# Query items kept in memory by column of head: loads of 8 KB rows, and one store for each of three parts

## What is computed

```python
x = x + attn(layernorm(x))
x = x + ffn(layernorm(x))

# attn
qkv = h @ Wqkv                      # 512 query columns, 16 key, 16 value
scores = einsum('bqhd,bkd->bhqk', q, k) * 16 ** -0.5
scores = where(causal, scores + slopes * (pos_k - pos_q), NEG_INF)
probs = softmax(scores)
attn = einsum('bhqk,bkd->bqhd', probs, v) @ Wo

# ffn: base layer, and the two best of 8 experts of rank 16
result = h @ W_base.T + b_base
delta  = sum over the two best experts of route_w * (h @ A_e.T) @ B_e.T
```

## Time and profile before

| what | value |
|---|---|
| time, median of 3 runs | 699.22 us (697.58 to 699.97) |
| the profiled execution | 698.62 us, span of its instructions 696.9 us |
| busy: PE / DVE / ACT / POOL | 673.5 / 552.3 / 360.7 / 216.5 us |
| granted clock of TensorE | 0.999 of full speed |
| loads of items (L504) | 96 DMAs of 128 KB, median 5.4 us from issue to landing |
| stores of items (L489) | 16 DMAs of 384 KB, median 4.4 us |

### The profile page before, as it was taken

How to read it: one execution, slowest core, us unless ns; L and a number is a source line. 1 busy time by engine, 2 the same in 40 slices (tenths; PEclk the granted TensorE clock), 3 DMA queues, 4 the chain that set the end, 5 groups by cost and what they waited for, 6 DMA issues and landing times.

```text
span 696.9 us, 13297 instructions
## 1 busy us (share of the span) xinstructions
PE 673.5 (97%) x4326; PEld 308.8 (44%) x4326; DVE 552.3 (79%) x1794; ACT 360.7 (52%) x519; POOL 216.5 (31%) x366
## 2 busy tenths in 40 slices
PE   7899999999999999999999999999999999999997
PEld 5444344544454444435443343343333455555553
DVE  6798989787989889898988989989881375656565
ACT  3325656666657667666666666666668411111111
POOL 0054323233341614234252231422431412222220
PEclk9999999999999999999999999999999999999999
DMA  9778108081411443080144843325200189600001
GB/s 243 161 146 141 42 6 143 28 153 27 152 61 44 65 85 118 2 132 34 40 70 89 117 75 67 52 46 95 48 18 34 64 123 177 151 31 31 30 31 60
DMA packets 43000, 56.32 MB, mean 81 GB/s; under 512 B 6697, under 2 KB 26281, under 8 KB 42801
## 3 DMA queue, kind: packets, MB, share of 16 engines
q1 hardware_dynamic: 40344, 51.27, 37.1%
q10 hardware_dynamic: 2592, 4.26, 1.8%
HBM read 35.72 MB, written 19.79 MB: 80 GB/s over the span
## 4 chain that ended last, share of the span: by engine, by line
PE 83%; DVE 9%; DMA 2%; ACT 2%; issue 1%; SPq 1%; POOL 0%; DVEq 0%; ACTq 0%; POOLq 0%
PE psum L784 20%; PE psum L736 18%; PE psum L766 13%; PE psum L812 8%; PE psum L834 7%; PE psum L682 7%; PE psum L763 5%; DVE psum L1170 3%; PE psum L829 2%; PE psum L844 2%; ACT work L976 2%; DVE negm L1175 1%; DMA x_sb<-in_x 1%; PE psum L821 1%; DMA arena<-q_dram 1%
## 5 line engine op out<-in xcount | busy, mean ns | idle before, releaser
L976 ACT ACTIVATE work<-psum 128x1024 f32<-128x1024 f32 (+1 forms) x320 | 288.9, 942 | 125.1 <-PE psum L766 106.6
L1170 DVE CUSTOM_DVE_ANT_0 psum<-psum,future 128x384 f32<-128x384 f32 (+3 forms) x512 | 238.0, 514 | 14.9 <-PE psum L736 12.8
L736 PE MATMUL psum<-k_op,arena 106*128 106x512 bf16 (+3 forms) x768 | 212.2, 328 | 9.3 <-DVE negm L1170 3.1
L1175 DVE TENSOR_REDUCE negm<-psum 128x1 f32<-128x512 f32 x256 | 168.7, 688 | 15.4 <-PE psum L736 11.2
L1345 POOL TENSOR_SCALAR_AFFINE_SELECT work<-work 128x512 f32<-128x512 f32 x128 | 81.5, 637 | 296.8 <-ACT work L976 296.8
L784 PE MATMUL psum<-work,v_op 128*32 128x512 f32 (+3 forms) x1536 | 163.4, 498 | 0.6 <-POOL work L1345 0.4
L766 PE MATMUL psum<-arena,k_op 109*128 109x512 bf16 (+3 forms) x640 | 157.4, 316 | 1.0 <-ACT work L976 0.8
L736 PEld LDWEIGHTS psum<-k_op,arena 106*128 106x128 bf16 x768 | 69.1, 97 | 127.9 <-DVE negm L1170 39.7
L682 PE MATMUL psum<-arena,wqkv_sb 128*128 128x256 f32 (+3 forms) x240 | 84.5, 452 | 1.2 <-ACT arena L894 1.2
L763 PE MATMUL psum<-arena,k_op 116*128 116x128 bf16 x512 | 84.1, 221 | 0.9 <-ACT work L976 0.9
L766 PEld LDWEIGHTS psum<-arena,k_op 109*128 109x128 bf16 x640 | 59.6, 98 | 43.1 <-ACT work L976 14.7
(11 more groups left out here) (90 smaller groups left out, 456.1 us busy)
## 6 DMA issues: line engine op xcount, KB each, us to landing
arena<-q_dram SPq DMA_DIRECT2D x96, 128.0 KB, 5.4
o_dram<-o_sb SPq DMA_DIRECT2D x32, 256.0 KB
q_dram<-arena SPq DMA_DIRECT2D x16, 384.0 KB, 4.4
arena<-o_dram SPq DMA_DIRECT2D x32, 128.0 KB, 4.5
arena<-rcp_dram SPq DMA_DIRECT2D x32, 128.0 KB, 4.8
out<-wqkv_sb ACTq DMA_DIRECT2D x16, 256.0 KB, 2.0
work<-in_x SPq DMA_DIRECT2D x3, 1024.0 KB, 16.9
x_sb<-in_x SPq DMA_DIRECT2D x8, 256.0 KB, 5.1
```

What stands on the lines that cost most here:

```text
L736: last = nc.tensor.matmul(bank[:, a * width:(a + 1) * width], q_op[0:ROW_MAX, bass.ds(col, P)], k_op[0:ROW_MAX, b, k0:k0 + width], start=T ...
L976: nc.scalar.activation(probs[:, n % 4, heads * hp:heads * (hp + 1), 0:w], src, ACT.Exp).then_inc(exp_done, 1)
L1170: last = nc.vector.tensor_tensor_reduce(keys, keys, future[:, CH - width:CH], -1.0, 3e38, ALU.add, ALU.min, negm[:, late, 0, j * QT + t:j ...
L1175: nc.vector.tensor_reduce(dst, psum[:, bank, 0:len(js) * width].rearrange("p (a k) -> p a k", a=len(js)), AX_X, ALU.max, negate=True).then ...
```

## The change

`q_dram` gets the shape (chunk, part, group, column, head, token). A load then takes one run of 8 KB (eight heads of 1 KB) for each of its 16 partitions, where it took eight runs of 1 KB. A store must put row h * 16 + d of the tile at place (d, h), which one DMA per part does: its memory side counts 8 heads, 16 columns, 512 tokens. The head part is issued as soon as ACT has written it, the other two after the split. The semaphore `q_stored` counts 48 for an item instead of 16.

```diff
-        q_dram = nc.dram_tensor("q_dram", (NCH, 3, D, CH), BF16, kind="Internal").ap()
+        q_dram = nc.dram_tensor("q_dram", (NCH, 3, PAIRS, DH, 2 * UH, CH), BF16, kind="Internal").ap()
...
             def store_queries(n):
                 c, m = Q_ITEMS[n]
-                if n < 2:
-                    sp.wait_ge(q_split_v, n + 1)
-                else:
-                    sp.wait_ge(q_split_p, n - 1)
                 if n:
-                    sp.wait_ge(q_stored, 16 * n)
-                sp.dma_start(q_dram[c, :, P * m:P * (m + 1)].rearrange("a r q -> r a q"),
-                             qpart[:, n % 4]).then_inc(q_stored, 16)
+                    sp.wait_ge(q_stored, 48 * n)
+                sp.wait_ge(q_hi_ready, n + 1)
+                for a in range(3):
+                    if a == 1:
+                        if n < 2:
+                            sp.wait_ge(q_split_v, n + 1)
+                        else:
+                            sp.wait_ge(q_split_p, n - 1)
+                    sp.dma_start(q_dram[c, a, m].rearrange("d h q -> h d q"), qpart[:, n % 4, a]).then_inc(q_stored, 16)
             def load_queries(n):
...
-                sp.wait_ge(q_stored, 16 * (n + 1))
+                sp.wait_ge(q_stored, 48 * (n + 1))
...
                 for r, (a, _) in enumerate(PARTS):
-                    sp.dma_start(q_op_pairs[DH * r:DH * (r + 1), c % 2, g].rearrange("d (h q) -> d h q", q=CH),
-                                 q_dram[c, a, g * P:(g + 1) * P].rearrange("(h d) q -> d h q", d=DH)).then_inc(q_in[n % 2], 16)
+                    sp.dma_start(q_op_pairs[DH * r:DH * (r + 1), c % 2, g],
+                                 q_dram[c, a, g].rearrange("d h q -> d (h q)")).then_inc(q_in[n % 2], 16)
...
                 if n >= 4:
-                    act.wait_ge(q_stored, 16 * (n - 3))
+                    act.wait_ge(q_stored, 48 * (n - 3))
```

## The result

| | before | changed |
|---|---|---|
| median of 6 runs each, same chip | 699.38 us (697.51 to 699.97) | 704.09 us (703.43 to 706.38) |
| ratio, 95% interval | | 1.0084 [1.007, 1.0098] |
| the profiled execution | 698.62 us, span 696.9 | 703.71 us, span 702.0 |
| granted clock, mean | 0.999 | 0.995 |

A forecast was written before the change was run, and what follows sets the result against it. PE bounds the kernel, busy 673.5 of 696.9 us. Item 0's +0.8 and the chain's +3.1 (4.5 - 0.4 - 1.0) make +3.9 on 698.6: 702.5, or 703.0 for a median; range 698.7 to 706.5.

The forecast's parts named there:

- slower: Whole kernel: chance 0.61 that the change makes it slower, against 0.33 for same and 0.06 for faster.
- the sum of 3.9: Whole kernel: +0.8 us at item 0 and +3.1 at the chain to unit 1, added to the profiled execution's 698.6.
- Loads, no change: Query item loads: 16 partitions limit them, not row size, so 8 KB rows cost 0; rival of faster loads 0.09.
- Stores use eight engines: Item stores: outermost count 8 gives eight engines, 165 GB/s, share near 0.5; rival that stores keep all engines 0.16.
- The price of a store, +1.5: Each item store takes 1.5 us longer, between +1.1 and +1.7; 4.5 us for three in the chain.
- the lower price of +1.1: Each item store at 165 GB/s takes 2.4 us against 1.3; rival of cheap stores, mostly covered, 0.17.
- crowd: Item stores: if eight engines crowd the same SBUF places, the rate is nearer 133 GB/s, +1.7 us per store.
- The place: Stores of items 3, 4 and 5 stand in series before unit 1's maximum rows; PE stands still 3.1 us there.
- the room before 71.47: Unit 1's maximum rows: 0.4 us of room between their load's landing and PE's first scores, taken off the loss.
- The cover of 1.0: Unit 1: DVE has other work at 72.42, so 1.0 us of PE's delay is taken as covered.
- Item 0, +0.8: Start: item 0's store ends 0.8 us later; PE already waits for these loads, so it is paid in full.
- Later items, 0: Ten more stores, one in a step and not in a chain, ahead of an early unit's maximum rows: cost 0.

The follow-up runs named there:

- long loads alone: Kernel before with W_q's columns permuted, so one store of 128 rows per item serves loads with 8 KB rows: 698.6 us, ratio 0.9995.
- the padded kernel: Kernel before, its order by head and 1 KB loads, a pad row per head and three 8 by 16 by 512 stores per item: 704.11 us, ratio 1.0074.
- The kernel kept busy: Changed kernel plus 14 matmuls, later overwritten, in front of unit 1's late scores to fill PE's wait: 703.4 us, ratio 1.007.
- that with 17 matmuls: Changed kernel plus 17 matmuls, later overwritten, in front of unit 1's late scores: 703.16 us, ratio 1.0054.
- one extra store: Kernel before plus one 384 KB store that nothing reads, between store 5 and unit 1's maximum rows: 699.48 us, ratio 1.0012.
- three stores on all engines: Kernel before, its layout and loads, each item stored by three DMAs of 128 rows, head part first: 698.9 us, ratio 1.0006.
- the broken chain: Changed kernel with unit 1's maximum rows moved ahead of store 5: 700.1 us, ratio 1.0014.

## Why the prediction held, step by step

The median of 704.09 lies 1.1 us above the 703.0, in the range, and slower was the likeliest side. In the profiled executions 5.1 us stand against the sum of 3.9.

- **Loads, no change: right.** The six landings of item 0 go from 2.9 to 5.6 us after issues that take 2.65 us in all, so they are 0.98 us apart against 1.04, at 145 GB/s. The kernel with long loads alone is as fast as before, and loads to 32 partitions move 1.6 to 1.8 times as much at the same share, which bears the reason out.
- **Stores use eight engines: right.** The share is 0.47 to 0.48, the padded kernel shows the same, and it alone gives the loss.
- **The price of a store, +1.5: too high, in a part that was guessed.** The rate that the lower price of +1.1 was worked out from (165 GB/s) is what is seen (154 to 165), so the eight blocks don't crowd. Taken were 4.5 us for the three, measured are 3.3 (up to 3.9 in the other executions): 0.67 and 0.71 where data moves under the issues, 1.94 at store 5. So the first two cost less than even the lower price, which isn't explained, and the third more: there the issues, costed at 0.38 and as lying under data, count in full, at 0.58 each.
- **The place: right.** The chain starts 0.5 us later (load 2 at 50.07 against 49.57), takes 3.3 more, and its end is 3.8 later (73.32 against 69.50). Its load then lands 1.60 us on, which makes the room before 71.47 - 69.50 - 1.60 = 0.37 us, predicted 0.4. Of 3.8, less 0.37, 3.45 arrive at PE. Breaking the chain at store 5 takes away most of the loss.
- **The cover of 1.0: right in kind, 0.8 in size.** The kernel kept busy shows 3.47 us turned into 2.66, that with 17 matmuls 3.7 into 2.9, and one extra store a wait of 0.75 turned into 0.02.
- **Item 0, +0.8: the store's price came, its way to PE did not.** From the end of the split to the first load it is 2.74 us before (20.38 to 23.12) and 3.41 in the changed kernel (19.60 to 23.01), so the store costs +0.7. But the split ended 0.8 us earlier in this execution, and the last load landed 5.6 us after its issue against 5.9; so the first slot is 0.47 us earlier, and PE's wait there 0.83 instead of 1.42. The late slots wait 0.5 for a query item instead and are 0.2 late. The step that failed is "paid in full": it took the end of the split and the landing of the loads as fixed. Why the split came earlier isn't shown, and the change need not be the reason: the kernel with long loads alone, which stores as before, has it at 19.58 too, and its first slot 0.3 us ahead of the changed kernel's. The first slot varies from 30.50 to 32.49 in the executions with before's stores and loads, and from 30.97 to 33.14 in those of the changed kernel and its edited versions at full clock.
- **The clock: left out.** The sum took PE's standing still at its length less the cover. Measured is 0.2 at the start, plus 3.25 less 0.8 of wait, plus 2.5 at the 1.2 GHz level: 5.15. Without the clock it is 2.65, 1.25 less than forecast: the stores were 1.2 too dear and item 0 0.6, while the chain began 0.3 later than unit 0's scores show and the cover was 0.2 smaller. That the sum came near is luck: two kinds of error had opposite signs. The trace of before couldn't show it here, since PE had no wait of this size in the run after its start.
- **Later items, 0: right.** The lag is constant from 82 us to the end.

## What to carry to other kernels

When a DMA is reshaped, count the outermost rows of both sides: here a store whose memory side counts 8 ran on half the engines, although it read 128 partitions. Change the order of the data where it is made (here the weights' columns) rather than in the DMA, and merge loads so that each fills more partitions (the loads ran faster here; what that alone gains was not resolved). When a change can add a wait of PE, look for the chain of landings that has the least room, and reckon that a stop of some 3 us can bring the clock down and then cost more than its length, while one under 1 us may cost nothing.

## What the runs showed of the hardware

- In all four traces in which PE stood without matmuls for 3.1 to 3.7 us in front of unit 1's scores, the granted clock fell to the 1.2 GHz level for some 3 to 7 us. It fell at a time between 1.6 us before the end of the wait and 1.4 us after it, and this added 1.4 to 2.5 us. After 0.75 us at the same place it did not fall. With unused matmuls in the gap it stayed at 1.00.
- Near 384 us, behind PE's 1.3 us of idleness, the clock fell in the profiled executions of three kernels (three stores on all engines, the broken chain, one extra store) and not in that of before, and took 1.2 us where it did. The kernel with the broken chain has it in its profile (clock in the last but two columns):

```profile
380.00:384.00 4.00, 2.53 (x25) 1.10 (x25) 3.03 (x11) 1.62 (x2) 2.59 (x7) 0.98 0.00 0
384.00:386.00 2.00, 2.00 (x14) 0.73 (x7) 1.94 (x10) 0.00 (x0) 0.00 (x0) 0.50 0.06 14
```

- SP's issue of a store of 8 by 16 by 512 took 0.57 to 0.65 us, of 128 by 3 by 512 0.38 and of 128 by 512 0.32 to 0.48.
- DMAs to 16 partitions moved 116 to 145 GB/s with a share of 0.94 to 1.15, with rows of 1 KB (129, 133), 2 KB (129) and 8 KB (116, 145); to 32 partitions 219 to 242.
